# A routed expert stage whose threshold search is split: one expert alone at four bits a round, the second beside the first blocks

## The reference, cut to what matters

```python
x = x + xattn(layernorm(x), ctx, ctx, mask, Wq, bq, Wk, bk, Wv, bv, Wo, bo)   # B=8, S=512, D=512, 16 heads
# second half: experts choose their tokens, N = 4096 tokens, E = 8 experts, F = 2048
xf = layernorm(x).reshape(N, D)
route_prob = softmax(xf @ Ws + bs).T                  # (E, N)
k = N // E                                            # 512 tokens for each expert
route_vals, routes = top_k(route_prob, k)
xin = xf[routes]
h = gelu(einsum('ekd,edf->ekf', xin, W1) + b1[:, None, :])
out = (einsum('ekf,efd->ekd', h, W2) + b2[:, None, :]) * route_vals[..., None]
x = x + zeros((N, D)).at[routes.reshape(-1)].add(out.reshape(-1, D))
```

## Time and profile before

| what | value |
|---|---|
| time, median of 3 runs | 1624.9 us (1621.7 to 1627.7) |
| the profiled execution: its own time | 1619.5 us |
| its span in the trace | 1617.7 us, mean granted TensorE clock 0.992 |
| busy shares | PE 96%, PE weight loads 71%, DVE 71%, ACT 58%, POOL 25% |

### The profile page before, as it was taken

One profiled execution on the slowest core, in us unless ns is written; L12 is line 12 of the kernel. 1 busy time (PEld: TensorE's weight loads), 2 busy tenths in 40 slices (PEclk: granted clock), 3 DMA queues, 4 the chain that ended last, 5 costly groups with the idle time before them and its releaser, 6 DMA issues.

```text
span 1617.7 us, 22176 instructions
## 1 busy us (share of the span) xinstructions
PE 1553.6 (96%) x7714; PEld 1151.6 (71%) x7714; DVE 1144.0 (71%) x2034; ACT 942.3 (58%) x2119; POOL 407.9 (25%) x448
## 2 busy tenths in 40 slices
PE   7999999999999999999986999999999999999998
PEld 5667566676666767666544777878888888888886
DVE  7787978879788797886846688774655555464644
ACT  5899898998989989899862222222222222232321
POOL 6220211202112021120300511327070514334100
PEclk9999999999999999999998999999999999999999
DMA  5653745637446374563522424316253524343440
GB/s 182 181 168 91 228 128 160 181 87 225 136 152 183 93 220 141 156 172 93 171 80 67 135 99 129 103 63 189 78 163 105 157 90 146 116 122 120 112 123 26
DMA packets 133638, 217.26 MB, mean 134 GB/s; under 512 B 19484, under 2 KB 53424, under 8 KB 133528
## 3 DMA queue, kind: packets, MB, share of 16 engines
q1 hardware_dynamic: 116568, 173.76, 34.4%
q0 software_dynamic: 16960, 42.09, 10.1%
HBM read 157.45 MB, written 57.82 MB: 133 GB/s over the span
## 4 chain that ended last, share of the span: by engine, by line
PE 68%; DVE 16%; DMA 6%; ACT 4%; issue 3%; POOL 1%; SPq 1%; ACTq 0%; POOLq 0%; DVEq 0%
PE ps_gen L933 8%; PE ps_gen L934 8%; PE ps_gen L935 8%; PE ps_gen L2160 7%; PE ps_gen L2162 6%; PE ps_gen L2161 6%; PE ps_gen L1994 5%; PE ps_gen L1962 5%; PE ps_gen L2006 4%; DVE nmax L1538 4%; PE ps_gen L1944 2%; PE ps_gen L1945 2%; PE ps_gen L1946 2%; DVE stat L1438 2%; DMA x_in<-in_ctx 2%
## 5 line engine op out<-in xcount | busy, mean ns | idle before, releaser
L1538 DVE TENSOR_REDUCE nmax<-ps_gen 128x1 f32<-128x512 f32 x512 | 332.9, 683 | 76.0 <-PE ps_gen L1962 74.4
L1337 ACT ACTIVATE ps_gen<-ps_gen,nmax 128x512 f32<-128x512 f32 x512 | 345.9, 684 | 49.2 <-DVE nmax L1538 45.6
L1408 ACT ACTIVATE gel<-ps_gen,b_cols 128x512 f32<-128x512 f32 x128 | 88.3, 690 | 481.1 <-PE ps_gen L935 473.1
L1347 ACT ACTIVATE p_ring<-ps_gen 128x512 f32<-128x512 f32 x512 | 293.5, 616 | 29.4 <-PE ps_gen L1994 25.0
L1824 DVE TENSOR_TENSOR gel_lo<-gel,gel_hi 128x512 fp32r<-128x512 f32 x126 | 87.1, 691 | 253.2 <-ACT gel_hi L1409 253.2
L2160 PE MATMUL ps_gen<-w_hi,gel_hi 128*128 128x512 f32 x504 | 198.9, 395 | 3.4 <-DVE gel_lo L1824 3.4
L2162 PE MATMUL ps_gen<-w_hi,gel_lo 128*128 128x512 f32 x504 | 197.0, 391 | 0.0
L1994 PE MATMUL ps_gen<-qst,kst 99*128 99x512 f32 x512 | 193.0, 419 | 4.0 <-DMA qst<-by_row 2.7
L2161 PE MATMUL ps_gen<-w_lo,gel_hi 128*128 128x512 f32 x504 | 196.7, 390 | 0.0
L933 PE MATMUL ps_gen<-hT_hi,w_hi 128*128 128x512 f32 x504 | 196.3, 389 | 0.0
L934 PE MATMUL ps_gen<-hT_lo,w_hi 128*128 128x512 f32 x504 | 196.1, 389 | 0.0
(11 more groups left out here) (233 smaller groups left out, 2767.7 us busy)
## 6 DMA issues: line engine op xcount, KB each, us to landing
w_raw<-in_L_ffn_W SPq DMA_DIRECT2D x128, 512.0 KB, 4.4
kst<-qk_rows SPq DMA_DIRECT2D x93, 256.0 KB, 4.4
qst<-qk_rows SPq DMA_DIRECT2D x93, 256.0 KB, 4.0
x_in<-in_x POOLq DMA_DIRECT2D x60, 256.0 KB, 4.4
out_x<-x_in SPq DMA_DIRECT2D x32, 256.0 KB, 2.5
qk_rows<-kT_hi SPq DMA_DIRECT2D x31, 256.0 KB, 2.5
qk_rows<-kT_lo SPq DMA_DIRECT2D x31, 256.0 KB, 2.6
qk_rows<-qT_hi SPq DMA_DIRECT2D x31, 256.0 KB, 2.1
```

The costliest lines, as they stand in the source:

```text
L1337: e.activation(psum[:, :], psum[:, :], ACT.Exp, bias=nmax[g % 2][:, c], scale=-1.0, accum_out=den[g % 2][:, c]).then_inc(drained_sem("max" ...
L1347: e.activation(p_ring[n % NP_][:, :], ps("score", g, kt, h)[:, :], ACT.Exp, scale=-1.0).then_inc(drained_sem("score", g, kt, h), 1)
L1538: e.tensor_reduce(nmax[g % 2][:, h * TB + t:h * TB + t + 1], ps("max", g, h, t)[:, :], AX.X, ALU.min).then_inc(s_min, 1)
```

## The change

FIRST becomes expert 0 alone, with 4 bits a round (8 rounds, the last overlapping the one before it by two bits). A new group SECOND holds expert 1, also with 8 rounds. For both, `ask` compares in two halves, each with its own count of `s_asked`, and `count` waits for each half. The rounds of SECOND are laid out as follows: 0 and 1 while the rows of expert 0 are fetched; 2 to 4 between the row tiles and weight splits of the start; the rest, its marks, ranks and list at blocks 0 to 4. `write_idx((1,))`, and with it the gather of expert 1, goes from block 1 to block 4. `hot_high` gets a wait for what DVE has issued before it. `turn_blocks`, `rows_hi` and `rows_lo` go one block later: transposes at j = 10 to 13, high and low parts at j = 11 to 14. TensorE's `keep_busy(12)` behind the first list becomes 2 + 4 + 4. The core of the diff:

```diff
-        FIRST, REST = (0, 1), tuple(range(2, E))
-        BITS = {FIRST: 3, REST: 2}
-        SHIFTS = {g: list(range(30 - BITS[g], -1, -BITS[g])) for g in (FIRST, REST)}
+        FIRST, SECOND, REST = (0,), (1,), tuple(range(2, E))
+        BITS = {FIRST: 4, SECOND: 4, REST: 2}
+        SHIFTS = {g: list(range(30 - BITS[g], -1, -BITS[g])) for g in (FIRST, SECOND, REST)}
+        for g in (FIRST, SECOND):
+            SHIFTS[g].append(0)
...
-        HOT_AT = {0: (1,), MARK_AT + 3: (2, 3), MARK_AT + 7: (4, 5), MARK_AT + 11: (6, 7)}
+        HOT_AT = {MARK_AT + 3: (2, 3), MARK_AT + 7: (4, 5), MARK_AT + 11: (6, 7)}
...
+        def search_bank(group):
+            return ps_first if group == SECOND else ps_den
+
+        def count_bank(group, k):
+            return ps_gen[5] if group == SECOND and k < BEFORE else search_bank(group)
+
+        BEFORE = 3
...
# scalar_program
-                if ex + 1 < E and NF - 6 <= j < NF - 2:
-                    rows_hi(ex + 1, j - (NF - 6))
+                if ex + 1 < E and NF - 5 <= j < NF - 1:
+                    rows_hi(ex + 1, j - (NF - 5))
...
# vector_program, ask
+                halves = 1 if group == REST else 2
+                for n in range(halves):
+                    ts = slice(n * NT // halves, (n + 1) * NT // halves)
+                    size = [P, NT // halves, ne, nc_ - 1]
+                    e.tensor_tensor(ind_v[:, ts, :, :], ...
+                                    ).then_inc(*(mark() if group == REST else (s_asked, 1)))
...
             def hot_high(exps):
                 on.wait_ge(s_listed, listed_before(exps))
+                on.wait_ge(s_sel, n_sel)
...
+            def second_before(i):
+                if i in (1, 2):
+                    answer(SECOND, BEFORE + 2 * i)
+                if i == 1:
+                    ask(SECOND, BEFORE + 3)
+                if i == 2:
+                    mark_chosen(SECOND)
+                if i == 3:
+                    slots(SECOND)
+                    hot_low((1,))
+                if i == 4:
+                    write_idx((1,))
+
+            def second_behind(i):
+                if i in (0, 1):
+                    answer(SECOND, BEFORE + 2 * i + 1)
+                    ask(SECOND, BEFORE + 2 * i + 2)
+                if i == 2:
+                    keep_totals(SECOND)
+                if i == 3:
+                    hot_high((1,))
...
             write_idx((0,))
+            ask(SECOND, 0)
+            for k in range(2):
+                answer(SECOND, k)
+                ask(SECOND, k + 1)
...
             rows_lo(0, 0)
             rows_lo(0, 1)
             early_w1_lo(0)
+            answer(SECOND, 2)
+            ask(SECOND, 3)
             rows_lo(0, 2)
             rows_lo(0, 3)
             early_w2_lo(0)
+            answer(SECOND, 3)
+            ask(SECOND, 4)
             early_w1_lo(1)
             early_w2_lo(1)
             gelu_lo(0)
             for i, (ex, j) in enumerate(order):
+                second_before(i)
                 if i + 1 < len(order):
                     gelu_lo(i + 1)
+                second_behind(i)
...
-                if ex + 1 < E and NF - 7 <= j < NF - 3:
-                    turn_blocks(ex + 1, j - (NF - 7))
                 if ex + 1 < E and NF - 6 <= j < NF - 2:
-                    rows_lo(ex + 1, j - (NF - 6))
+                    turn_blocks(ex + 1, j - (NF - 6))
+                if ex + 1 < E and NF - 5 <= j < NF - 1:
+                    rows_lo(ex + 1, j - (NF - 5))
...
# tensor_program, count
-                on.wait_ge(s_asked, rounds_before(group) + k + 1)
                 parts = 1 if group == REST else 4
                 for n in range(parts):
-                    last = e.matmul(ps_den[:, 0:part], ...
+                    on.wait_ge(s_asked, asked_before(group) + (k + 1 if group == REST else 2 * k + 1 + n // 2))
+                    last = e.matmul(count_bank(group, k)[:, 0:part], ...
...
+            def second_before(i):
+                if i in (0, 1):
+                    count(SECOND, BEFORE + 2 * i + 1)
+                if i == 2:
+                    total(SECOND)
+
+            def second_behind(i):
+                if i in (0, 1):
+                    count(SECOND, BEFORE + 2 * i + 2)
+                if i == 2:
+                    rank_all(SECOND)
+                if i == 3:
+                    list_slots((1,))
...
             list_slots((0,))
-            keep_busy(12)
+            keep_busy(2)
+            count(SECOND, 0)
+            keep_busy(4)
+            count(SECOND, 1)
+            keep_busy(4)
...
             for tt in range(3):
                 turn_rows(tt)
+                if tt == 2:
+                    count(SECOND, 2)
...
             for m in range(2):
                 up_half(m, 1, True)
                 up_half(m, 1, False)
+            count(SECOND, 3)
             up(2)
             for i, (ex, j) in enumerate(order[:BODY]):
                 if i > 1:
                     up(i + 1)
                 route_beside(i)
+                second_before(i)
                 down(i)
+                second_behind(i)
```

More of the change, by code:

```diff
@@ L880, in attention_moe_kernel, with asked_before, nth, units_of @@
         MARK_AT = 2 + len(SHIFTS[REST])
-        HOT_AT = {0: (1,), MARK_AT + 3: (2, 3), MARK_AT + 7: (4, 5), MARK_AT + 11: (6, 7)}
+        HOT_AT = {MARK_AT + 3: (2, 3), MARK_AT + 7: (4, 5), MARK_AT + 11: (6, 7)}
         def rounds_before(group):
-            return 0 if group == FIRST else len(SHIFTS[FIRST])
-        def pairs_of(group):
-            return [(e0, e0 + 1) for e0 in group[::2]]
+            return sum(len(SHIFTS[g]) for g in (FIRST, SECOND, REST)[:(FIRST, SECOND, REST).index(group)])
+        def asked_before(group):
+            return {FIRST: 0, SECOND: 2 * rounds_before(SECOND), REST: 2 * rounds_before(REST)}[group]
+        def nth(group):
+            return (FIRST, SECOND, REST).index(group) + 1
+        def units_of(group):
+            return [group] if len(group) == 1 else [(e0, e0 + 1) for e0 in group[::2]]
+        def columns(group, n):
+            w = MARKS * len(units_of(group)[0])
+            return slice(n * w, (n + 1) * w)
+        def search_bank(group):
[3 more added lines that the diff above has]
+        BEFORE = 3
         def listed_before(exps):
@@ L2063, in count @@
                 on.wait_ge(s_tables, TABLES)
-                on.wait_ge(s_asked, rounds_before(group) + k + 1)
                 parts = 1 if group == REST else 4
                 for n in range(parts):
-                    last = e.matmul(ps_den[:, 0:part], lhsT=ones_h[:, :], rhs=ind[:, n * part:(n + 1) * part], start=(n == 0), stop=(n == parts - 1))
+                    on.wait_ge(s_asked, asked_before(group) + (k + 1 if group == REST else 2 * k + 1 + n // 2))
+                    last = e.matmul(count_bank(group, k)[:, 0:part], lhsT=ones_h[:, :], rhs=ind[:, n * part:(n + 1) * part], start=(n == 0), stop=(n == parts - 1))
                 last.then_inc(s_counted, 1)
@@ L2075, in keep_busy, with marks_of @@
                     e.matmul(psum[:, :], lhsT=w1s[0][0][:, 0, 0:P], rhs=w1s[0][0][:, 0:2, :], start=True, stop=True)
-            def pair_marks(e0):
-                return marks[:, e0:e0 + 2, :, :].rearrange("p e m t -> p (e m t)")
+            def marks_of(unit):
+                return marks[:, unit[0]:unit[0] + len(unit), :, :].rearrange("p e m t -> p (e m t)")
             def total(group):
-                psum = ps_first if group == FIRST else ps_den
-                on.wait_ge(s_marked, 1 if group == FIRST else 2)
-                for n, (e0, _) in enumerate(pairs_of(group)):
-                    last = e.matmul(psum[:, n * P:(n + 1) * P], lhsT=pair_marks(e0), rhs=ones_h[:, :], start=True, stop=True)
+                psum = ps_den if group == REST else ps_first
+                on.wait_ge(s_marked, nth(group))
+                for n, unit in enumerate(units_of(group)):
+                    last = e.matmul(psum[0:MARKS * len(unit), n * P:(n + 1) * P], lhsT=marks_of(unit), rhs=ones_h[:, :], start=True, stop=True)
                 last.then_inc(s_totalled, 1)
             def rank_all(group):
-                on.wait_ge(s_totals, 1 if group == FIRST else 2)
-                for n, (e0, _) in enumerate(pairs_of(group)):
-                    c = slice(n * P, (n + 1) * P)
-                    e.matmul(ps_den[:, c], lhsT=tri[:, :], rhs=pair_marks(e0), start=True, stop=False)
-                    last = e.matmul(ps_den[:, c], lhsT=totals[:, c], rhs=after[:, :], start=False, stop=True)
+                on.wait_ge(s_totals, nth(group))
+                psum = search_bank(group)
+                for n, unit in enumerate(units_of(group)):
+                    w = MARKS * len(unit)
+                    c = columns(group, n)
+                    e.matmul(psum[:, c], lhsT=tri[:, :], rhs=marks_of(unit), start=True, stop=False)
```

(3 more changed lines are left out.)

54 lines of the change are left out of this document (26 added, 28 removed).

## The result

The changed kernel took 1642.5 us (median of 4 runs, 1640.3 to 1645.6) beside 1624.6 us for the kernel before (4 runs): a ratio of 1.0104, 95% interval 1.0075 to 1.0133. It is slower by 17.9 us.

The account below looks back on a forecast made before the run. The search's TensorE-DVE round trips and then TensorE's own full stream were taken to set the end. Terms -4.5 + 3.2 + 5.35 + 3.9 - 0.8 + 1.1 + 4.0 = +12.25 us gave a median of 1637 us, range 1625 to 1643.

Parts of the forecast that it names:

- rival 4: DVE doesn't catch up after block 5; every count up to block 9 waits a few tenths: +3, 1640 us, chance 0.08.
- The search: Expert 0's search: two rounds fewer save 4.0 us, halves nothing at full clock; -4.5 us, bounds -3.2 and -6.
- Rival 3: The shorter search gives more: early halves use idle TensorE, full clock comes sooner; about -2, 1635 us, chance 0.1.
- The sum 0.6 us worse: Search by the skill page alone: the second half costs 0.08 us more in each of 8 rounds.
- `up(2)`: Start of expert 0: TensorE waits 3.1 us for `early_w1_lo(1)`, behind round 3's pair; +3.2 us, bounds 2.8 to 3.6.
- Blocks 0 to 4: Four more counts, expert 1's own `total` and rank, and waits of TensorE for DVE; +5.35 us, bounds 2.5 and 7.5.
- `up(16)`: Expert 0 to 1: last low part stands behind `gelu_lo(15)`, round 12 of REST and a transpose; 3.9 us late.
- `up(32)`: Expert 1 to 2: the 3.45 us `gel_lo` wait goes, one of some 4.5 us comes; -0.8 us.
- Rival 2: Later rows aren't late: `up(16)` and `up(32)` don't wait; -0.6, 1624 us, chance 0.17 with other ways of much shorter waits.
- The clock: Low clock behind waits: 1.6 us each at `up(16)` and `up(32)`, 0.8 at `up(2)`; +4.0 us, bounds 0 and 4.8.
- Rival 1: The waits come as forecast but TensorE keeps full clock behind them; +8.2, 1633 us, chance 0.15.
- Experts 2 to 7: Five expert changes: low part behind another transpose, low part and `gelu_lo`, 0.2 us late each; +1.1 us, bounds 0 and 2.

Follow-up runs that it names:

- a4: Changed kernel with one compare of 480 elements a round instead of two halves; 1644.6 us, ratio 1.0114.
- d1: The changed kernel run again, unaltered, on a third chip; 1642.6 us, ratio 1.0102.
- a3: Kernel before, with nothing changed but the rows a block later; 1635.6 us, ratio 1.0057.
- b1: Changed kernel plus unused matmuls to keep TensorE at work, 16 ahead of `up(16)` and 19 ahead of `up(32)`; 1641.4 us, ratio 1.0104.
- a2: Changed kernel with `early_w1_lo(1)` and `early_w2_lo(1)` ahead of round 3's `answer` and `ask`; 1636.3 us, ratio 1.0073.
- a1: Changed kernel with the transposes and low parts of the later rows back in their old blocks; 1631.1 us, ratio 1.0040.
- d2: c2 run again, on a third chip; 1622.5 us, ratio 0.9980.
- c1: Kernel before, with expert 2's rows alone a block later and the lists of experts 4 to 7 at blocks 34 and 50; 1620.7 us, ratio 0.9973.
- c3: c2 with the w1 half of `split_piece` 2 moved to the end of block 0; 1629.3 us, ratio 1.0026.
- c2: Changed kernel, expert 2's rows alone a block later, lists of experts 4 to 7 at blocks 34 and 50, early weight splits before round 3's answer; 1626.9 us, ratio 1.0023.

## Why the prediction was right, and where its steps were off

The forecast was 1637 us (1625 to 1643) and slower; it came to 1642.5, half a microsecond below the upper bound and outside the 1631 to 1642 that the prediction gave its likeliest case; what it kept the rest up to 1643 for, rival 4, didn't come. So the range held by a little luck. The waits came where they were forecast, nearly at their lengths; what was too small were the clock and several small terms. The 5.3 us by which the sum fell short of 17.6 are made up as follows.

**The search**, -4.5: measured -4.5. Behind the right sum stand two errors that nearly cancel, which is luck: with one compare a late round takes 2.15 us (a4), where I had 2.02, and the halves, which I had at nothing, give 0.1 of it back, so that it is 2.05. Rival 3, in which the halves bring a further 2 us, is out. The sum 0.6 us worse, which the prediction worked out from the Trainium skill (VectorE: DVE Perf Modes, the section on the TRN2 errata), is out too: the pair took the 0.73 us that follow if half of the second fixed part is hidden.

**`up(2)`**, +3.2: the wait was 2.98 where 3.1 was forecast, released by the second `w_lo` as the prediction had it (its line is L1894 here; L1843, which the prediction names, is its line in the kernel before). With the count of round 3 ahead of it, from 906.38 to 909.75, that is 3.4 us. Of the other 1.3 us of this part 0.7 are `keep_busy` at low clock, which d1 shows to be an accident of one execution, and 0.1 is the new wait in `hot_high`; the rest wasn't taken apart.

**Blocks 0 to 4**, +5.35: the waits were 1.44, 0.73, 0.55 and 0.88, together 3.6 where I had 4.0, and `total` was late by 0.73 and not 1.2. What was mis-sized is what the added matmuls cost: with the waits and the clock taken out of this part of the balance (11.7 - 3.6 - 3.9 - 1.6), 2.6 us are left where I had 1.35. Measured from start to start on TensorE, the four counts add 1.2 us and `total` and rank 0.4 (1.1 and 0.25 forecast). The late count took 0.60 us [the line at 919.03] where with one compare it took 0.38 (a4), as its second half waits for the second compare. About 0.5 more lies behind them: the first matmul of `up` or `down` behind each starts its successor after 0.31 to 0.34 us, instead of 0.23. The prediction has no term for that. The last 0.5 stays open.

**`up(16)`**, +3.9: 3.92 measured. **`up(32)`**: the `gel_lo` wait went and one of 4.80 took its place, where I had some 4.5; without the clock, 1.2 - 1.6 = -0.4 for a forecast of -0.8. a3 shows that the two are the shift's own doing, whatever the search does: +10.5 us, which my terms put at 3.9 + 1.6 - 0.8 + 1.6 + 1.1 = 7.4. Of the other 3.1 the low clock is 1.8 (there `up(16)` lost 2.4 us to it and `up(32)` 2.6, instead of 1.6 each) and the five later steps, below, 0.9; 0.4 stays open. Rival 2, in which the later rows aren't late, is refuted by it.

**The clock**, +4.0: too low twice. Behind `up(2)` I counted half; it fell fully, 1.6. Behind `up(32)` all twelve matmuls ran near half clock (0.50 over 4 us): from their start at 1106.04 to the gelu at 1111.47 were 5.43 us, before 2.92 from 1084.64 to 1087.56, so 2.5 and not 1.6. At `up(16)`, 1.6 as said. Together 5.7, above the upper bound of 4.8 as well. Rival 1 is refuted by the windows, and b1 shows the cost by its absence. The Trainium skill (TensorE: Matmul & The Clock Gate, "HAM oscillation") says that each long enough wait sends the array back to half clock and the matmuls behind it start cold. The traces agree: all three waits were long enough, that of 2.98 us too; at 1.44 us the clock stayed. I had given the row of 3.45 us too sharp an edge.

Yet 1.6 and 2.5 us are no prices of a short and a long wait. From the first matmul behind the wait to the gelu that needs them, a2 lost 2.5 us at `up(16)`, behind 3.92 us of idle, and 1.5 at `up(32)`, behind 4.79, the other way round than after; a3 lost 2.4 and 2.6 (behind 3.92 and 4.37), a4 1.4 and 2.6 (behind 3.92 and 5.14). Timelines of PE and ACT in a2, both places; 5.49 and 4.41 us, where the kernel before has 3.01 and 2.92:

```profile
995.70 0.76 PE L956 MATMUL ps_gen<-hT_hi,w_hi 128*128 128x512 f32 x1 [3.92 <-DVE hT_lo L1869]
...
1001.19 0.69 ACT L1432 ACTIVATE gel<-ps_gen,b_cols 128x512 f32<-128x512 f32 x1 [9.03 <-PE ps_gen L958]
...
1097.79 0.77 PE L956 MATMUL ps_gen<-hT_hi,w_hi 128*128 128x512 f32 x1 [4.79 <-DVE hT_lo L1869]
...
1102.20 0.69 ACT L1432 ACTIVATE gel<-ps_gen,b_cols 128x512 f32<-128x512 f32 x1 [8.84 <-PE ps_gen L958]
```

The wait at block 27, from which the prediction took its 1.6, shows it too: in a1, at 3.62 us, the twelve matmuls of `down(27)` took 5.28 us from start to start, 2.5 more than at full clock. So waits of 2.98 us and more cost 1.4 to 2.6 us of clock, not ordered by their length, and one row gave only one draw from that range. What decides the cost these runs don't show.

**Experts 2 to 7**, +1.1: I had 0.2 a place. Timeline of ACT at the step from block 47 to 48, where the pitch of two gelus shows the delay:

```profile
1193.12 0.69 ACT L1432 ACTIVATE gel<-ps_gen,b_cols 128x512 f32<-128x512 f32 x1 [3.65 <-PE ps_gen L958]
...
1198.95 0.69 ACT L1432 ACTIVATE gel<-ps_gen,b_cols 128x512 f32<-128x512 f32 x1 [4.05 <-PE ps_gen L958]
```

5.83 us, where the kernel before has 5.44 (1169.16 to 1174.60): 0.4 at each of five steps, 2.0 us, at the upper bound. a1, with the rows back, has 5.44 again.

Rival 4, DVE never catching up, did not come: two counts of REST waited under a microsecond, at 946.32 and 992.25.

Summed, the terms that were off are: clock +1.7, matmuls of the early blocks +1.3, experts 2 to 7 +0.9, `up(2)` +1.4 (half of it an accident), `up(32)` +0.4, early waits -0.4: 5.3.

The change without its two faults is d2: 755.9 us of stretch against 758.2, ratio 0.9980. But c1, which has the old search with expert 1 in it, is at 753.9, so nothing shows that searching expert 0 alone gains anything. Between the same instructions of the two traces, d2 less c1:

| part | d2 less c1 |
|---|---|
| first `cand` to start of `hot_a` | -4.4 |
| to `up(2)` | +0.9 |
| to `up(16)` | +5.4 |
| to `up(32)` and to the end | +0.1 |

The split shortens the chain by 4.4 us and puts back 6.2, in counts and waits in TensorE's full stream, although c1 has the pause of ScalarE in it and d2 has not. What gains in both is that the wait ahead of block 27 goes. The profiled executions put c1 2.0 us ahead (those of after and d1, one program, differ by 0.3); the medians put it only 0.2 ahead (3.7 and 3.5 us under their kernels before), and the two ratios, taken on different chips, overlap. In times their order stays open.

## What to carry to other kernels

Ask of every step that is moved later on a shared engine what is queued ahead of it in the new place: here one block later meant a transpose, a low part and a whole search round ahead of the last `hT_lo`, and cost 3.9 us at one expert; moved later for expert 2 alone, whose rows land late, with two lists moved out of the way, they made the kernel 0.3% faster than before (c1). Price a stall of TensorE with the matmuls behind it: waits of 2.98 to 5.14 us cost 1.4 to 2.6 us more in clock here. And work taken off a latency chain isn't free where it is put if that engine's stream is full.

## What the runs showed that I had not expected

- The clock fell behind a wait of 2.92 us (c3) and of 2.98 us, and stayed at 1.00 behind 1.44 us, and 1.94 us (c3). What the low clock cost then didn't follow the length of the wait: 1.6 us behind 3.92 and 2.5 behind 4.80 in after, 2.5 behind 3.92 and 1.5 behind 4.79 in a2.
- Two compares of 240 on DVE were busy for 0.73 us together, one of 480 for 0.66 us; yet the round with two was 0.1 us shorter.
- On one chip a gelu of ScalarE started 1.9 to 4.3 us late, in four profiles of four, with nothing in the program for it to wait for; each time beside or just behind POOL's gathers of `prob` rows for expert 1, in c1 three blocks earlier with them. The same program had it on one chip and not on another (c2 and d2): c2's median was 2.5 us above that of the kernel before in its series, d2's 3.5 below. The stretches of the two differ by 4.6 us.
- The first half of the program, which no kernel changed, ended anywhere from 859.5 to 871.9 us.
